# Stage three of an attention and MLP kernel: another order of TensorE's blocks, and VectorE's h made one step sooner

## The reference, cut to what matters

```python
def _layernorm(x, g, b):
    mu = jnp.mean(x, axis=-1, keepdims=True)
    var = jnp.var(x, axis=-1, keepdims=True)
    return (x - mu) * jax.lax.rsqrt(var + LN_EPS) * g + b
...
    attn = jax.nn.softmax(sid_sim / D ** 0.5, axis=-1)
    attn_feat = jnp.einsum('bnm,bmd->bnd', attn, v)
    f_diff = (v - attn_feat) @ W_diff.T + b_diff + q
    h = _layernorm(f_diff, ln_g, ln_b)
    mlp = jax.nn.gelu(h @ W1.T + b1, approximate=False) @ W2.T + b2
    out = mlp + f_diff
    return _layernorm(out, ln_g, ln_b)
...
    x = x + _L0_xattn_ref(_layernorm(x, axis=-1), ctx_1024, ctx_1024, ...)
    x = x + _L0_ffn_ref(_layernorm(x, axis=-1), L0_ffn_weight, L0_ffn_bias)
```

## Time and profile before

| | us |
|---|---|
| median of 3 runs | 253.02 |
| range of the 3 runs | 253.01 to 253.81 |
| the profiled execution, time | 252.62 |
| the profiled execution, span | 250.7 |
| PE busy in the span | 212.1 (85%) |
| DVE busy | 221.9 (89%) |
| ACT busy | 216.3 (86%) |
| POOL busy | 191.1 (76%) |

### The profile page before, as it was taken

One profiled execution on the slowest core, in us unless ns is written; L12 is line 12 of the kernel. 1 busy time (PEld: TensorE's weight loads), 2 busy tenths in 40 slices (PEclk: granted clock), 3 DMA queues, 4 the chain that ended last, 5 costly groups with the idle time before them and its releaser, 6 DMA issues.

```text
span 250.7 us, 6047 instructions
## 1 busy us (share of the span) xinstructions
PE 212.1 (85%) x1777; PEld 181.2 (72%) x1777; DVE 221.9 (89%) x842; ACT 216.3 (86%) x780; POOL 191.1 (76%) x255
## 2 busy tenths in 40 slices
PE   3958765977498888999999999999999999998621
PEld 1847654766486666776879999998999999988610
DVE  2999999998899999999355889999999999999992
ACT  5699999998999999997987888899888777886673
POOL 2567756678899999975695896969699698666773
PEclk9997999799889999999999999999999999999975
DMA  6767645540000000003037379996987899987614
GB/s 187 179 196 208 178 135 142 156 116 11 3 3 0 3 3 1 3 4 42 3 41 84 26 100 131 122 131 113 149 131 121 129 141 125 131 126 119 93 43 126
DMA packets 50816, 23.52 MB, mean 94 GB/s; under 512 B 9312, under 2 KB 50656, under 8 KB 50784
## 3 DMA queue, kind: packets, MB, share of 16 engines
q0 software_dynamic: 15856, 7.87, 28.5%
q1 hardware_dynamic: 34784, 15.21, 22.9%
q10 hardware_dynamic: 144, 0.07, 0.1%
HBM read 9.37 MB, written 4.19 MB: 54 GB/s over the span
## 4 chain that ended last, share of the span: by engine, by line
POOL 29%; ACT 14%; DVE 14%; issue 13%; PE 5%; DVEq 0%; ACTq 0%; POOLq 0%
POOL F L444 8%; POOL xrstd L486 7%; POOL orstd L479 5%; POOL F L500 5%; ACT LN_c L627 3%; ACT q_c L617 3%; DVE LN_c L932 2%; DVE q_c L920 2%; POOL HALFK L512 2%; DVE F L954 2%; ACT lT_c L661 1%; ACT E_c L637 1%; PE bank L1140 1%; ACT vT_c L652 1%; DVE F L981 1%
## 5 line engine op out<-in xcount | busy, mean ns | idle before, releaser
L1140 PEld LDWEIGHTS bank<-W2T,TQK 128*128 128x128 f32 x512 | 62.9, 191 | 4.6 <-ACT TQK L601 1.2
L1140 PE MATMUL bank<-W2T,TQK 128*128 128x128 f32 x512 | 64.5, 277 | 1.0 <-ACT TQK L601 1.0
L601 ACT ACTIVATE TQK<-bank,b1c 128x512 f32<-128x512 f32 (+1 forms) x68 | 43.0, 664 | 5.4 <-PE bank L1133 4.8
L486 POOL TENSOR_TENSOR xrstd<-xvar,pow_c 128x4 f32<-128x4 f32 (+1 forms) x17 | 18.6, 1094 | 19.8 <-DVE xvar L809 19.8
L381 POOL TENSOR_TENSOR xrstd<-xvar,pow_c 128x4 f32<-128x4 f32 x16 | 17.0, 1060 | 20.8 <-DVE xvar L809 20.8
L1131 PE MATMUL bank<-hTh,W1h 128*128 128x512 f32 (+1 forms) x68 | 30.0, 442 | 0.6 <-DVE hTl L899 0.6
L444 POOL DMA_DIRECT2D F<-rows x17 | 26.0, 1529 | 2.8 <-DVE E_c L894 2.8
L1070 PE MATMUL bank<-WdT,vT_c 128*128 128x128 f32 x128 | 21.3, 319 | 6.7 <-DVE F L851 3.6
L1132 PE MATMUL bank<-hTl,W1h 128*128 128x512 f32 (+1 forms) x68 | 26.0, 382 | 0.0
L1133 PE MATMUL bank<-hTh,W1l 128*128 128x512 f32 (+1 forms) x68 | 25.9, 380 | 0.0
L1070 PEld LDWEIGHTS bank<-WdT,vT_c 128*128 128x128 f32 x128 | 18.7, 225 | 9.6 <-ACT vT_c L571 8.3
(11 more groups left out here) (134 smaller groups left out, 661.2 us busy)
## 6 DMA issues: line engine op xcount, KB each, us to landing
F<-rows POOLq DMA_DIRECT2D x29, 256.0 KB, 4.7
LN_c<-in_ctx_dram SPq DMA_DIRECT2D x16, 256.0 KB, 2.9
X<-in_x_dram SPq DMA_DIRECT2D x16, 256.0 KB, 3.1
out_dram<-F SPq DMA_DIRECT2D x15, 256.0 KB, 2.4
LN_c<-in_L_xattn_W_dram SPq DMA_DIRECT2D x1, 256.0 KB, 3.3
lT_c<-in_L_xattn_W_dram SPq DMA_DIRECT2D x1, 256.0 KB, 3.6
F<-rows POOLq DMA_DIRECT2D x2, 128.0 KB, 4.8
out_dram<-F SPq DMA_DIRECT2D x2, 128.0 KB, 1.8
```

The lines of the kernel that those rows point to most:

```text
L486: pool.tensor_tensor(buf(xrstd, x1, G), buf(xvar, x1, G), pow_c[:, 0:x1.g], ALU.pow).then_inc(x1_rstd, 1)
L601: act.activation(hid(m, j), m1_bank(m, j), ACT.Gelu, bias=b1c[:, j:j + 1]).then_inc(gelu_ready, 1)
L1140: last = pe.matmul(M2_B[m.buf][:, i * D:(i + 1) * D], hid(m, j)[:, i * D:(i + 1) * D], W2T[:, j * D:(j + 1) * D], start=(j == 0 and i == 0 ...
```

## The change: three engines' order within a step

On PE, `turn_h` moves ahead of the two first-layer blocks, and the second layer's first block moves behind the first layer's last one. On ACT, `upper_half` moves ahead of the first two gelus. On DVE, `take_h` of the next piece (n+1) stands behind `lower_half` of piece n, ahead of `result` and `quantise`, instead of at the start of the next step. No instruction is added or removed, and POOL's and SP's programs are as before.

```diff
 # ACT
             def phase3(at):
                 h, m, o, c = at(0), at(1), at(2), at(3)
 
+                if h.live and h.n > 1:
+                    upper_half(h)
                 if m.live and m.n > 0:
                     gelu(m, 0)
                     gelu(m, 1)
                 if is_piece(m, 1):
                     act.wait_ge(wf_ps, 1)
                     act.activation(WfT[:, :], XQ_B[:, 0:D], ACT.Copy).then_inc(wf_sb, 1)
-                if h.live and h.n > 1:
-                    upper_half(h)
 # DVE
                 h, o, x1, y = at(0), at(2), at(3), at(5)
-                if h.live:
-                    if h.n >= EARLY:
-                        dve.wait_ge(frstd, EARLY + h.n // 2)
-                    if h.n > 1:
-                        take_h(h)
                 if o.live:
                     output(o)
...
                 if h.live and h.n > 1:
                     lower_half(h)
+                h = at(-1)
+                if h.live and h.n >= EARLY:
+                    dve.wait_ge(frstd, EARLY + h.n // 2)
+                    take_h(h)
                 if y.live:
                     result(y)
 # PE
                 h, m, q = at(0), at(1), at(4)
+                if h.live and h.n > 1:
+                    turn_h(h)
                 if m.live and m.n > 0:
                     mlp1(m, 0)
                     mlp1(m, 1)
-                if h.live and h.n > 1:
-                    turn_h(h)
...
                     if m.n > 0:
                         mlp1(m, 2)
+                    mlp1(m, 3)
                     mlp2(m, 0)
-                    mlp1(m, 3)
                     mlp2(m, 1)
```

## The result

The changed kernel takes 256.92 us (median of 5 runs, 254.61 to 257.58) against 253.02 us before (252.37 to 253.81). The ratio is 1.0138, with a 95% interval of 1.011 to 1.0166: +3.9 us, where +1.3 had been forecast. The profiled execution of the changed kernel is its fastest, 254.61 us. That gap of 2.3 us between its own profile and its median turned out to be a part of the answer.

The account below looks back on a forecast made before the run. Bound: DVE's first real output at 134.25 and its pace from there, held up a little by POOL. 1.47 - 0.60 + 0.74 - 0.29 = +1.32 us on 253.02 gave 254.3, range 253.0 to 256.3.

Parts of the forecast that it names:

- The start of the stage, +1.47 us: PE idles until piece 2's late h, its transposes now first, so piece 1's output starts at 135.72 instead of 134.25.
- the clock in that gap: Rival: PE's clock falls in the new 2 us gap before piece 2's transposes, costing 2 us: 256.3; chance 0.06.
- take_h ahead of quantise, -0.60 us: On DVE, output starts right after quantise; 0.60 us gained once, in the first POOL-bound step.
- the forecast meeting (+0.41): In step 4, POOL's power falls on DVE's take_h and starts 0.41 us later than due.
- Meetings, +0.74 us: POOL's x1_power meets DVE's take_h in norm steps: +0.41 in step 4, +0.11 in three later; bounds 0 and 2.8.
- End, -0.29 us: In step 15, piece 16's take_h fills DVE's 0.29 us wait for POOL; the second such wait, in step 16, stays.
- PE's and ACT's order, nothing: The new order within the step shortens only a path on PE and ACT that DVE doesn't wait for: no gain.
- loop through ACT: Rival: cast and upper half before the first gelu make ACT's loop the bound, +2.4 us, 256.7; chance 0.07.
- `take_h` of the steady part was stretched: Rival: POOL stretches DVE's take_h, half of thirteen losing 0.5 us, 257; chance 0.04.
- the waits for POOL did not vanish: Rival, faster: take_h fills all 2.7 us of DVE's waits, 251.8 with the late start; chance 0.11.
- only seven waits: Claim that DVE, after piece 1's output at 134.25, has seven waits, 2.7 us together, all before quantise for POOL's xrstd.

Follow-up runs that it names:

- the filler: The changed kernel with fourteen transposes of the identity, result unused, on PE ahead of piece 2's transposes: 255.45 us, ratio 1.0091 to the kernel before.
- step 2's order: The kernel before with the change's order on PE and ACT in step 2 and nowhere else: 255.48 us, ratio 1.0101.

## Why the prediction was wrong, step by step

**The start of the stage, +1.47 us: right.** It is 7.30 - 5.89 = 1.41 us in the profile after, and the filler shows it again (7.31). The working from the earlier trace rows held: the six matmuls that had covered the wait stood behind it.

**The step that failed: the clock in that gap was left out of the sum.** It stood among the rivals with a chance of 0.06, as 2 us and 256.3. It happens in most executions and costs 1.55 us. The argument against it was that the gap "is half as long and lies in dense work". The row it went by, the 0.78 with 4 us idle, couldn't carry that, and it was not the only one on the matter. Stage one of the same trace of before has a fall behind an idle stretch shorter than the one to come, PE first and then its stretches of 2 us:

```profile
19.29 1.12 PE L1088 MATMUL bank<-ident,LN_c 128*128 128x128 f32 x4 [1.82 <-DMA LN_c<-in_ctx_dram]
```

```profile
18.00:20.00 2.00, 0.71 (x4) 0.81 0.81 255
20.00:22.00 2.00, 2.00 (x11) 0.50 0.83 241
```

The granted clock is at 0.50 again from 44 to 46 us, where no single gap ahead reaches 1 us, and from 68 to 70 us, behind gaps of 1.68, 1.59 and 0.78 us. There PE was busy for 0.4 to 1.4 of every 2 us before the fall, while here the work ahead of the gap is dense, and after single gaps of 1.16 and 1.18 us (at 16.11 and 28.24) the clock stayed at 1.00. So these rows don't decide the case, but they make the fall anything but remote: it should have stood beside the 1.47 as a term with bounds from 0 to 2 us. Without it the forecast for a usual execution is short by 1.5 us.

**take_h ahead of quantise, -0.60 us: right.** Output 1 to output 4 is 0.64 us shorter. The quantises came at 140.72 and 147.82, with 141.1 and 148.8 forecast: the stage began 0.30 us earlier, and in step 4 the forecast meeting (+0.41) didn't occur: the power listed from 146.50 took 1.28 us, as before (1.29), and quantise waited 0.21 us. POOL's way there even got 0.17 us shorter, since L510 took 0.71 us instead of 0.88. The wait for piece 2's output is 0.34 us (0.3 forecast).

**Meetings, +0.74 us: right in kind, placed on the wrong operation, and mis-sized.** From output 4 to output 14 the steady part lost 1.50 us where meetings of 0.33 were forecast (three times 0.11; the 0.41 of step 4 came to nothing). The 0.29 that the end of the stage was to gain lies in this stretch too and didn't come, so the 1.50 stands against a forecast of 0.04. Without the meetings the stretch takes 70.97 us, less than before, so they account for all of it. The listed partner was `take_h` at the power. It is already past there. By the order of time the partners are `result`, which `take_h` has pushed 0.60 us later onto the power (+0.34 in a full norm step), and the sum of `residual`, which the very gain of the step above has moved 0.60 us sooner onto L510 (+0.39). My sum looked at one operation of POOL's way and one DVE operation beside it; all five operations of that way and all DVE operations with two SBUF operands had to be laid side by side. The upper bound of 2.8 did hold it.

The rule of the Trainium skill (SBUF — State Buffer, "Who interferes with whom") pointed the right way, and here the run without a second SBUF operand in three of DVE's operations agrees with it: 2.06 us less from output 4 to output 14, with the same number of instructions.

**End, -0.29 us: not seen.** Output 14 waits 0.29 us for PE in the profile after, where before the wait was at the quantise ahead of it. What `take_h` filled came back as a wait for the second layer.

**PE's and ACT's order, nothing: right for this kernel** (254.36 against 254.17 us). Under POOL's limit it is hidden, and freed of it it may bring 0.4 us.

**The sum.** Against the profiled execution, which escaped the clock's fall, 253.9 was forecast and 254.61 measured: +0.7, which is -0.30 (earlier stages), -0.06, -0.04, +0.76 and +0.31. Against the median the clock's 1.55 us come on top, and the earlier stages are left out, since they vary from one execution to the next: 1.41 + 1.55 - 0.64 + 1.50 = 3.8 of the 3.9 us measured. Run apart, step 2's order gives +1.0% and DVE's part +0.35%; together they are the whole change's 1.4%.

**The other rivals.** No loop through ACT became the bound of the changed kernel: DVE waits for the second layer three times in the whole stage, once for 4.6 us and twice for about 0.3. No `take_h` of the steady part was stretched: all of 512 columns from 130.12 us on have 0.68 us, but one with 0.71. (That rival's 257 was too low by its own terms: half of thirteen times 0.5 is 3.2 us, 257.6.) And the waits for POOL did not vanish, they grew from 2.7 to 3.2 us. The "only seven waits" of the working left out two for ACT behind 246 us (1.45 and 0.69 us); they are the same after the change, as is the whole stretch behind output 14.

## What to carry to other kernels

Before an instruction that waits is moved ahead of work that doesn't, look up how long it waits in the first iteration, not only in the steady ones: the matmuls that stood ahead of it were the cover, and their loss was paid twice here, as 1.4 us of idle and as 1.55 us of a lower clock. Before a new gap on TensorE is called harmless, read the granted clock over the whole trace, and not only in the stage that the change touches; where no row is like the gap, it is an unknown cost with bounds, not a rival. When an operation moves on one engine, lay every operation of the other engine's critical way beside every operation that it shifts, since it isn't only the moved one that meets something new.

## What the runs showed of the hardware

- A single idle stretch of 1.98 to 1.99 us on TensorE was followed by a granted clock of 0.50 (1.2 GHz of 2.4) in three of four profiled executions that had it, and one of 1.82 us in looser work was in the kernel before. In the kernel with step 2's order alone the granted clock was 0.83, 0.50, 0.81 and 1.00 in the four stretches of 2 us from 128 us on. The price was 1.55 us. With fourteen transposes in the gap (idle 0.46 us) it didn't fall in the profiled execution, and none of the four runs has the long time.
- POOL operations of four and eight columns lose up to 0.55 us when they meet a DVE operation of 512 columns with two SBUF operands: L510 took 0.71 to 0.72 us alone and 1.26 to 1.27 under the sum, L512 1.66 and 2.04, and the power lost 0.34. The opposite holds for wide ones: a DVE operation of 512 columns takes 0.69 us alone and 1.7 to 1.8 us beside a POOL add of the same size. The small POOL operations did not lengthen DVE's of 512 columns by more than 0.04 us (0.68 to 0.72).
- The two POOL DMA issues of a norm step kept their 1.32 us listed in the kernel before and in the changed one.
